# One Macaron block on one core: five changes of order, and the FFN normalisations on ScalarE

## The reference, cut to what matters

```python
x = L0_attn_x                                    # (32, 256, 128) f32
x = x + 0.5 * ffn(layernorm(x))                  # f1
x = x + mamba(layernorm(x))
x = x + 0.5 * ffn(layernorm(x))                  # f2, the same weights
# ffn: logits = x @ Wg + bg; e = argmax over 8 experts
#      y = gelu(x @ W1[e] + b1[e]) @ W2[e] + b2[e]
# mamba: xz = rmsnorm(x) @ in_proj.T -> x_path, z; x_path = silu(causal conv4(x_path) + b)
#      dt, B, C from x_path; dt = softplus(dt @ dt_proj.T + b)
#      h = exp(dt * A) * h + dt * x * B;  y = sum_n h * C + D * x   (16 states, 256 channels)
#      (y * silu(z)) @ out_proj.T + x
```

## Time and profile before

| | us |
|---|---|
| median of 3 runs (lowest, highest) | 1329.93 (1327.08, 1342.4) |
| the profiled execution, its own time | 1330.48 |
| its span, first to last instruction | 1328.7 |
| busy: PE, DVE, ACT, POOL | 1142.2, 1060.7, 857.7, 1067.7 |
| mean granted clock of TensorE | 0.897 |

### The profile page before, as it was taken

How to read it: one execution, slowest core, us unless ns; L and a number is a source line. 1 busy time by engine, 2 the same in 40 slices (tenths; PEclk the granted TensorE clock), 3 DMA queues, 4 the chain that set the end, 5 groups by cost and what they waited for, 6 DMA issues and landing times.

```text
span 1328.7 us, 16290 instructions
## 1 busy us (share of the span) xinstructions
PE 1142.2 (86%) x5188; PEld 579.9 (44%) x5188; DVE 1060.7 (80%) x1713; ACT 857.7 (65%) x1159; POOL 1067.7 (80%) x900
## 2 busy tenths in 40 slices
PE   6886868799999898999989898998989896969588
PEld 3432324244535444544445454454435443524246
DVE  2317989988898988888988988888888889888930
ACT  2327475777768687767768677767768686574531
POOL 1365999998998998889998998899898989897810
PEclk9877979899989998999989999999989997878689
DMA  3060333332141333233141333233141323232000
GB/s 95 0 232 2 135 95 122 111 121 103 59 164 37 135 106 133 90 118 123 58 154 47 135 105 123 100 123 117 42 150 59 135 98 135 96 134 98 0 9 16
DMA packets 60405, 130.02 MB, mean 98 GB/s; under 512 B 7744, under 2 KB 26864, under 8 KB 52128
## 3 DMA queue, kind: packets, MB, share of 16 engines
q1 hardware_dynamic: 60320, 128.98, 28.1%
HBM read 106.94 MB, written 22.02 MB: 97 GB/s over the span
## 4 chain that ended last, share of the span: by engine, by line
PE 59%; DVE 21%; ACT 8%; issue 6%; POOL 5%; SPq 0%; DMA 0%; DVEq 0%; ACTq 0%; POOLq 0%
PE PY L594 17%; PE PH L563 12%; PE G L550 9%; DVE dA L926 8%; PE Y L606 7%; DVE hb L924 4%; PE PH L562 4%; PE G L641 3%; DVE hb L930 3%; PE G L542 2%; PE dA L576 2%; POOL hb L1112 2%; DVE stat L905 2%; ACT hs L751 1%; ACT dA L775 1%
## 5 line engine op out<-in xcount | busy, mean ns | idle before, releaser
L1112 POOL TENSOR_TENSOR hb<-dtx_rep,bs 128x1024 f32<-128x1024 f32 x256 | 598.7, 2359 | 0.0
L926 DVE TENSOR_TENSOR_SCAN dA<-dA,hb 128x512 f32<-128x512 f32 x352 | 429.1, 1219 | 23.8 <-ACT dA L775 16.8
L775 ACT ACTIVATE dA<-dt_rep,A 128x512 f32<-128x512 f32 x512 | 343.7, 690 | 115.9 <-DVE hb L930 97.6
L594 PE MATMUL PY<-W,hs 128*128 128x128 f32 x2048 | 298.6, 289 | 0.0
L594 PEld LDWEIGHTS PY<-W,hs 128*128 128x128 f32 x2048 | 261.9, 196 | 82.8 <-issue 72.1
L731 ACT COPY hs<-PH 128x512 f32<-128x512 f32 x232 | 135.2, 583 | 237.7 <-PE PH L563 235.0
L563 PE MATMUL PH<-xnT,W 128*128 128x512 f32 x464 | 280.5, 688 | 0.0
L930 DVE TENSOR_TENSOR hb<-dA,cs 128x512 f32<-128x512 f32 x352 | 243.5, 692 | 24.8 <-DVE dA L926 0.5
L1120 POOL TENSOR_TENSOR hb<-hb,cs 128x1024 f32<-128x1024 f32 x80 | 188.7, 2359 | 85.0 <-DVE hb L924 85.0
L924 DVE TENSOR_TENSOR_SCAN hb<-dA,hb 128x512 f32<-128x512 f32 x160 | 186.4, 1206 | 8.9 <-ACT dA L775 6.8
L606 PE MATMUL Y<-hb,Sel 128*32 128x512 f32 x1024 | 161.3, 707 | 29.5 <-POOL hb L1120 19.6
(11 more groups left out here) (97 smaller groups left out, 1247.6 us busy)
## 6 DMA issues: line engine op xcount, KB each, us to landing
dtx_rep<-dtx_rows SPq DMA_DIRECT2D x32, 1024.0 KB, 6.5
dt_rep<-dt_rows SPq DMA_DIRECT2D x32, 1024.0 KB, 8.0
bs<-bc_rows SPq DMA_DIRECT2D x64, 256.0 KB, 3.6
cs<-bc_rows SPq DMA_DIRECT2D x64, 256.0 KB, 4.2
dtx_rows<-dtx SPq DMA_DIRECT2D x32, 256.0 KB, 2.5
dt_rows<-dt SPq DMA_DIRECT2D x32, 256.0 KB, 2.6
X<-in_x SPq DMA_DIRECT2D x16, 256.0 KB, 3.0
out<-X SPq DMA_DIRECT2D x16, 256.0 KB, 2.4
```

Of the source, the lines that this page charges most:

```text
L594: last = nc.tensor.matmul(PY[:, P * j:P * (j + 1)], hs[:, w, e, P * j:P * (j + 1)], W2[:, e, :], start=False, stop=e == E - 1 and j == J - 1)
L775: nc.scalar.activation(dA[u % NA][:, :], dt_rep[:, h, g, :], ACT.Exp, scale=A[:, h, g, q:q + 1]).then_inc(decay, 1)
L926: nc.vector.tensor_tensor_scan(a, a, x_in_hb, 0.0, ALU.mult, ALU.add).then_inc(scan, 1)
L1112: nc.gpsimd.tensor_tensor(hb[:, s % HR], dtx_rep[:, h, 2 * m:2 * m + 2, :], bs[:, q, None, :].broadcast_to([P, 2, CH]), ALU.mult).then_inc ...
```

## The change

- The output product goes to Y instead of G0, from (3, 1) to (2, 2); its addition on DVE goes from 3.5 to 3.25, between two units. The first sum of an iteration waits until Y has been read again (`out_read`).
- The one-hot of f1 on DVE goes from 1.0 to 1.25, behind the first unit of slot 1; its transposes on PE from (6, 0) to (5, 1).
- Decay 2 is made in slot 15, ahead of the gelus of f1, and decay 14 in slot 5, ahead of dt0's reads; state_bx(5) in slot 2 instead of 3. x's silu comes before z's. dt0's reads go from 5.5 to 6.0.
- The first product of f1's expert 4 goes to PY, at (10, 3); the places of most other first products and copies move.
- The normalisations of f1 and f2 become four `ACTIVATE` Identity on ACT with scale rstd and bias -m * rstd, a small product more on POOL (`shift`). Their places are 14.5 and 7.5 in the steady plan, and slot 1 in iteration -3.

```diff
-BANK = {"ln_f1": 0, "z0": 0, "out": 0, "bc": 0, "dt0": 0, "gate_f2": 0, "ln_p": 0, "x0": 0,
-        "gate_f1": 1, "z1": 1, "dt1": 1, "oh_f1": 1, "ln_f2": 1, "oh_f2": 1, "x1": 1}
+BANK = {"ln_f1": 0, "z0": 0, "bc": 0, "dt0": 0, "gate_f2": 0, "ln_p": 0, "x0": 0,
+        "gate_f1": 1, "z1": 1, "dt1": 1, "oh_f1": 1, "ln_f2": 1, "oh_f2": 1, "x1": 1, "out": None}
...
 STEADY = Plan(
-    stages=[("ln_f1", 0, 0), ("gate_f1", 0, 2), ("z0", 1, 0), ("z1", 1, 2), ("out", 3, 1), ("bc", 4, 1), ("dt1", 5, 0),
-            ("dt0", 5, 1), ("oh_f1", 6, 0), ("ln_f2", 9, 0), ("gate_f2", 10, 1), ("oh_f2", 12, 0), ("ln_p", 13, 0),
+    stages=[("ln_f1", 0, 0), ("gate_f1", 0, 2), ("z0", 1, 0), ("z1", 1, 2), ("out", 2, 2), ("bc", 4, 1), ("dt1", 5, 0),
+            ("dt0", 5, 1), ("oh_f1", 5, 1), ("ln_f2", 9, 0), ("gate_f2", 10, 1), ("oh_f2", 12, 0), ("ln_p", 13, 0),
             ("x1", 14, 0), ("x0", 14, 1)],
-    w1=[*[(0, e, *at, 3) for e, at in experts((8, 0, 8, 0), (9, 0, 9, 0), (10, 0, 10, 0), (10, 2, 10, 3), (11, 0, 11, 0),
-                                              (12, 0, 12, 0), (13, 0, 13, 0), (14, 1, 14, 0))],
-        *[(1, e, *at) for e, at in experts((15, 0, 15, 0, -1), (15, 1, 15, 0, -1), (15, 3, 15, 3, -1), (0, 2, 0, 1, -2),
-                                           (2, 0, 2, 0, -2), (3, 0, 3, 0, -2), (4, 0, 4, 0, -2), (5, 0, 6, 0, -2))]],
+    w1=[*[(0, e, *at, 3) for e, at in experts((8, 0, 8, 0), (9, 0, 9, 0), (10, 0, 10, 0), (10, 2, 10, 3), (10, 3, 10, 3),
+                                              (11, 1, 11, 0), (12, 0, 12, 0), (13, 0, 13, 0))],
+        *[(1, e, *at) for e, at in experts((14, 1, 14, 0, -1), (15, 0, 15, 0, -1), (15, 1, 15, 1, -1), (15, 3, 15, 3, -1),
+                                           (1, 0, 0, 2, -2), (2, 0, 2, 1, -2), (3, 0, 3, 0, -2), (4, 1, 4, 1, -2))]],
     w2=[*[(0, e, s, 1, 2) for e, s in experts(5, 6, 7, 7, 8, 8, 9, 9)],
         *[(1, e, *at) for e, at in experts((13, 1, -2), (14, 1, -2), (15, 1, -2), (15, 2, -2), (0, 1, -3), (0, 1, -3),
                                            (1, 1, -3), (2, 1, -3))]],
-    act={"silu": 3.0, "bc": 4.5, "dt1": 5.5, "dt0": 5.5, "soft": 6.0, "gelu_f2": 10.5, "ln_f2": 9.5, "ln_p": 13.5,
+    act={"silu": 3.0, "bc": 4.5, "dt1": 5.5, "dt0": 6.0, "soft": 6.0, "norm_f2": 7.5, "norm_f1": 14.5, "gelu_f2": 10.5, "ln_f2": 9.5, "ln_p": 13.5,
          "taps": 14.0, "gelu_f1": 15.5},
-    dve={"gate_f1": 1.0, "gated1": 1.5, "y_f2": [(3.5, -3)], "out": 3.5, "stats_f2": 4.0, "oh_f1": 7.0, "gated0": 9.5,
+    dve={"gate_f1": 1.25, "gated1": 1.5, "y_f2": [(3.5, -3)], "out": 3.25, "stats_f2": 4.0, "oh_f1": 7.0, "gated0": 9.5,
          "y_f1": 10.0, "stats_p": 10.5, "gate_f2": 11.0, "stats_f1": 12.0, "oh_f2": 13.0, "tap01": 15.0, "tap2": 15.5},
-    pool={"root_f2": 5.5, "norm_f2": 6.0, "dt": 7.0, "dtx": 7.5, "root_p": 11.0, "norm_p": 12.0, "root_f1": 12.5,
-          "norm_f1": 13.0},
+    pool={"root_f2": 5.5, "dt": 7.0, "dtx": 7.5, "root_p": 11.0, "norm_p": 12.0, "root_f1": 12.5},
...
 FILL = {
-    -4: Plan(dve={"stats_f1": 0}, pool={"root_f1": 0, "norm_f1": 1}),
+    -4: Plan(act={"norm_f1": 0}, dve={"stats_f1": 0}, pool={"root_f1": 0}),
     -3: Plan(
...
-        act={"ln_f1": 0}, dve={"gate_f1": 0, "oh_f1": 1, "stats_f1": 2}, pool={"root_f1": 0, "norm_f1": 1},
+        act={"ln_f1": 0, "norm_f1": 1}, dve={"gate_f1": 0, "oh_f1": 1, "stats_f1": 2}, pool={"root_f1": 0},
...
-        act={"ln_f1": 0, "ln_p": 6, "taps": 7.5},
+        act={"ln_f1": 0, "ln_p": 6, "norm_f1": 6.5, "taps": 7.5},
...
-        act={"silu": 0, "bc": 2, "dt1": 3, "dt0": 3, "soft": 3.5, "ln_f1": 4.5, "ln_p": 10.5, "taps": 11.5, "gelu_f1": 15.5},
+        act={"silu": 0, "bc": 2, "dt1": 3, "dt0": 3, "soft": 3.5, "ln_f1": 4.5, "ln_p": 10.5, "taps": 11.5, "norm_f1": 12.5, "gelu_f1": 15.5},
...
-    w1=[(1, 3, 0, 0, 0, 0, -2), (1, 4, 0, 0, 0, 0, -2), (1, 5, 0, 1, 1, 0, -2), (1, 6, 1, 1, 2, 0, -2),
-        (1, 7, 2, 1, 3, 0, -2)],
+    w1=[(1, 4, 0, 0, 0, 0, -2), (1, 5, 0, 1, 1, 0, -2), (1, 6, 1, 1, 2, 0, -2), (1, 7, 2, 1, 3, 0, -2)],
...
-    act={"gelu_f2": 3.5, "ln_f2": 4.5},
+    act={"gelu_f2": 3.5, "norm_f2": 4.0, "ln_f2": 4.5},
...
+IN_PY = (0, 4)
+
+EARLY = {(15, 0): 2, (5, 1): 14}
+
+EARLY_B = {2: 5}
...
-                nc.tensor.matmul(PH[:, :], W1[:, e, :], xnT[:, w, :], start=False, stop=True).then_inc(ph_full, 1)
+                if in_py(it.plan, w, e):
+                    it.wait(pe, y_added[0], off - 1, 1, 1)
+                    bank, full = PY, py_full
+                else:
+                    it.wait_unit(pe, ph_free, w, e, 0)
+                    bank, full = PH, ph_full
+                nc.tensor.matmul(bank[:, :], Lm[:, e, :], ohT[:, w, (it.i0 + off) % 2, :], start=True, stop=False)
+                nc.tensor.matmul(bank[:, :], W1[:, e, :], xnT[:, w, :], start=False, stop=True).then_inc(full, 1)
 
...
                         it.wait(pe, y_added[0], 2, 1, 1) if it.has(2) else it.wait(pe, y_added[1], off - 1, 1, 1)
+                        if it.has(3):
+                            it.wait(pe, py_free, 0, 1, 1)
...
                 if k == 0:
-                    it.wait(pe, gated, off, HF, 0)
+                    it.wait(pe, out_read, off - 1, 1, 1)
...
-                    it.wait_free(pe, g_free, "out")
-                    b = BANK["out"]
                     for j in range(J):
                         for h in range(HF):
-                            last = nc.tensor.matmul(G[b][:, P * j:P * (j + 1)], y2[:, h, P * j:P * (j + 1)],
+                            last = nc.tensor.matmul(Y[:, P * j:P * (j + 1)], y2[:, h, P * j:P * (j + 1)],
                                                     Wo[:, h, :], start=h == 0, stop=h == HF - 1)
-                    last.then_inc(g_full[b], 1)
+                    last.then_inc(out_made, 1)
                 xsc = xs[:, (it.i0 + 1) % 2].rearrange("p h b l -> p h (b l)")
...
+            def normalize(it, w, off):
+
+                it.wait(act, rooted[w], off, 1, 1)
+                if it.has(off - 1):
+                    Iteration(it.i0 + off - 1 - OFF[f"ln_f{w + 1}"]).wait_read(act, g_free, f"ln_f{w + 1}")
+                for j in range(J):
+                    last = nc.scalar.activation(xn[:, w, j, :], X[:, it.tiles(off, j, 1), :].rearrange("p o h -> p (o h)"),
+                                                ACT.Identity, scale=rstd[:, w, j:j + 1], bias=shift[:, w, j:j + 1])
+                last.then_inc(normed[w], 1)
...
+                if in_py(it.plan, w, e):
+                    it.wait(act, py_full, 0, 1, 1)
+                    nc.scalar.copy(hs[:, w, e, :], PY[:, :]).then_inc(py_free, 1)
+                else:
+                    it.wait_unit(act, ph_full, w, e, 1)
+                    nc.scalar.copy(hs[:, w, e, :], PH[:, :]).then_inc(ph_free, 1)
 
...
                     it.wait(act, gated, -1, HF, HF)
-                    if it.i0 < 0:
-                        x_silu(it, c)
+                    x_silu(it, c)
                     for h in range(HF) if it.i0 >= 0 else (1, 0):
                         it.wait_full(act, g_full, f"z{h}")
                         b = BANK[f"z{h}"]
                         nc.scalar.activation(zs[:, c, h, :], G[b][:, :], ACT.Silu).then_inc(g_free[b], 1)
-                    if it.i0 >= 0:
-                        x_silu(it, c)
...
-                    if it.has(off):
+                    if it.has(off) and 2 * t not in EARLY.values():
                         make_decay(it, off, 2 * t)
...
-                    stages(it, s + 0.5)
+                    for k in range(2):
+                        if k:
+                            stages(it, s + 0.5)
+                        if (s, k) in EARLY and it.has(off):
+                            make_decay(it, off, EARLY[s, k])
...
-                last = nc.gpsimd.tensor_tensor(rstd[:, w, :], vt[:, w, :], half[:, :], ALU.pow)
+                nc.gpsimd.tensor_tensor(rstd[:, w, :], vt[:, w, :], half[:, :], ALU.pow).then_inc(pool_ln[w], 1)
+                it.wait(pool, pool_ln[w], off, m, 3)
                 if w < 2:
-                    last.then_inc(rooted[w], 1)
+                    nc.gpsimd.tensor_tensor(shift[:, w, :], neg[:, w, :], rstd[:, w, :], ALU.mult).then_inc(rooted[w], 1)
                     return
-                last.then_inc(pool_ln[w], 1)
...
-                    if it.has(off):
+                    if it.has(off) and t not in EARLY_B.values():
                         state_bx(it, off, t)
+                    if it.has(0) and s in EARLY_B:
+                        state_bx(it, 0, EARLY_B[s])
```

51 lines of the change are left out of this document (25 added, 26 removed).

## The result

The changed kernel takes **1356.69 us** (median of 4 runs, 1354.16 to 1362.11) against 1328.51 for the kernel before on the same chip: 1.0178 times, with a 95% interval of 1.0133 to 1.0222. It is slower by 1.8%; I had forecast 1324 and a range up to 1350. The profiled execution has a span of 1355.3 us against 1328.7, at a mean granted clock of 0.884 against 0.897.

The account below looks back on a forecast made before the run. No engine is full; the order between them bounds the loop, forecast at 73.9 us against 75.1. From 1330.48, -12 (loop) - 1 (early) - 5 (tail) + 10 (fill) + 2 (drain) gave 1324.5, median 1324 us, range 1293 to 1350.

Parts of the forecast that it names:

- The clock term: PE's slow stretch behind the hole after the gelus: 0.6 us a period, bounds 0 and 1.7.
- Leg A: Loop part from scan unit 3 on DVE to the first FFN's addition y_f1: 34.1 us, against 35.1 before.
- the transposes' hole: PE stands still 1.6 us ahead of f1's one-hot transposes, until dt1's second read frees the bank.
- The late copy: f1's four activations at 14.5 delay the copies of experts 1 and 2, hence decay 1: 0.9 us a period.
- Legs B and C: Loop from y_f1 to unit 31's end, 28.9 us, then to the next unit 3, 9.4 plus 0.9 for the copy.
- Fill: In iteration -3 ACT's normalisation waits for POOL's root, holding up all eight gelus: +10 us (8 to 12).
- early periods: Periods from 114 to 328 us: leg C gains 0.9, the dt1 wait takes back half to all; -1 us.
- Tail and drain: Tail saves scans and an output product wait, -5 us (-2 to -7); drain has norm_f2 behind both gelus, +2 (0 to 4).
- Rival 3: PE at 1.2 GHz after the 1.6 us hole before the transposes, late slow stretch every period: 1352 us, chance 0.15.
- Rival 1: PE waits for no bank in leg A, no slow stretch or late copy: loop 70.8, time 1293 us, chance 0.15.
- Rival 2: The clock holds behind the 2.55 us hole after the gelus: 0.6 off per period, 1318 us, chance 0.18.
- Rival 4: Nothing of the fill's wait shows, because PE's work there has slack: 1314 us, chance 0.05.

Follow-up runs that it names:

- kernel 6: kernel 1 plus two idle pairs (expert 5's first product of f1 repeated twice into the same bank) per steady iteration: 1326.8 us, ratio 0.998 to before.
- kernel 7: The kernel before plus two idle pairs, repeats of f1's expert 3 first product, per steady iteration: 1338.4 us, ratio 1.006 to before.
- kernel 4: The changed kernel plus one idle pair, f1's expert 5 first product made once more, per steady iteration: 1336.2 us, ratio 1.008 to before.
- kernel 5: kernel 2 plus two idle pairs (f1's expert 5 first product repeated twice) per steady iteration: 1308.7 us, ratio 0.984 to before.
- kernel 9: kernel 5 with the one-hot transposes of f1 back at slot 6: 1284.6 us, ratio 0.967 to before.
- kernel 10: kernel 6 with the one-hot transposes of f1 back at slot 6: 1293.4 us, ratio 0.973 to before.
- kernel 1: The changed kernel with iteration -3's normalisation on ACT moved from slot 1 to 8.5, behind the direct gelus: 1344.0 us, ratio 1.012 to before.
- kernel 2: The changed kernel with both normalisations back on POOL everywhere, leaving the order changes alone: 1326.8 us, ratio 0.998 to before.
- kernel 12: kernel 2 without the product in PY, f1's expert 4 back in its old bank: 1325.1 us, ratio 0.997 to before.
- kernel 11: kernel 2 with the one-hot transposes of f1 back at slot 6, no idle work: 1299.0 us, ratio 0.977 to before.
- kernel 8: kernel 1 with the one-hot transposes of f1 back at slot 6: 1328.1 us, ratio 1.000 to before.
- kernel 3: The kernel before with both normalisations on ACT (iteration -3's at slot 8.5), no order changes: 1348.7 us, ratio 1.014 to before.

## Why the prediction was wrong, by its own steps

**The clock term is the step that failed.** For the slow stretch behind the hole that follows the gelus I gave 0.6 us a period, with 0 and 1.7 as bounds. Without a slow stretch the whole change runs at 73.03 (kernel 6), where my legs sum to 34.1 + 28.9 + 9.4 + 0.9 = 73.3; with the stretches the period of after is 76.07. The term is 76.07 - 73.03 = **3.0 us**, and ten times 2.4 more is 24 us. The fault was in the bounds. I took the difference between the two periods of before, 75.9 and 74.2, as the full price of the slow clock; but the shorter of them also had a loss of 3.7, half of it behind this same hole, and the only period of that kernel without any took 73.0 (kernel 7). The upper end also took it that the stretch behind the hole would be as long as before's, 12 us; with a hole 0.3 shorter it was up to 17. That the clock is what costs the time, and is no mere sign of it, rests on the idle pairs (kernels 4, 5, 6, 9 and 10) and on the table of losses.

**Leg A, the transposes' hole, the output product.** Right: 33.5 us for 34.1, a hole of 1.78 for 1.6; no wait for zs. (The walk puts the second read of dt1 at +17.5 where its own terms add up to 17.3; the transposes came at 591.84 - 574.60 = 17.2.) The hole was on the loop at nearly its full length: 1.1 to 1.9 a period by the table of losses, and 1.5 between kernels 5 and 9 (72.26 and 70.75).

**The late copy.** Right: 0.9 forecast, 0.8 measured, in the place that was named. An activation takes 481 ns (0.50 forecast), four 1.65 us (1.7).

**Legs B and C.** 39.2 forecast without the clock. In the period of kernel 6 in which the clock holds, they take 39.5: right.

**Fill.** +10 forecast (8 to 12), +16.4 in the profile, 12.7 between the medians of after and kernel 1. The wait, the table load of 1.28 and the first gelu were within 0.4 us. What hangs on the wait is 12.0 us by the next iteration's one-hots (50.92 for 38.94), 2 more than forecast. The other 4.5 came between the one-hots of iterations -1 and 0, and are no price of the normalisations that I can show: this stretch took 36.0 to 37.3 us in six kernels and 40.6 to 42.5 in eight, and either place of the normalisation is found in both groups. The whole fill varies as much. With one and the same code for it iteration 0's one-hots were at 112.3, 117.5, 122.9, 123.0 and 123.1 (kernels 2, 12, 5, 9 and 11, normalisations on GpSimd), and with another at 112.5, 117.8, 118.3 and 123.5 (10, 8, 1 and 6, on ScalarE behind the gelus). So the 4.0 of kernel 3 lie within what varies by itself. Of its 7.1 in the early periods, which I had at -1, I can't say more: kernel 10 has only 0.8 more there than kernel 9, kernel 6 has 5.9 more than kernel 5. The Trainium skill's 2.66 us for a table switch ("ScalarE: Activation LUTs", section "What ACT_TABLE_LOAD costs") is not what makes up the difference: in after the load starts at 27.51 and the activation behind it at 28.80, 1.29 us.

**Tail and drain.** -4.1 for -5 and +2.9 for +2: right. The normalisations alone cost about 4 at the end (80.7 in kernel 1, 76.8 in kernel 2).

**The rivals.** Rival 3's second half happened (a late slow stretch in every period), at nearly twice its price; its first half did not: behind the hole of 1.78, where it put PE at 1.2 GHz, the clock stayed at 1.00. Its 1352 is near the measured time with half of the mechanism. Rival 1's loop of 70.8 is what kernel 9 has at a held clock, but only with the transposes moved back, the hole filled and the normalisations on GpSimd. Rival 2 fell: the clock was lower behind the 2.43 in every period. Rival 4 fell with kernel 1, where the fill's wait went and 12 us with it.

The sum with measured terms, in span (what the fill has over the forecast includes the 4.5 that vary by themselves): the forecast was 1328.7 - 6 = 1322.7. Over the nine periods the clock adds 9 x 2.4 = 21.6 and the legs take off 9 x 0.27 = 2.4; the tenth period's forecast gain of 1.2 lies in the stretches beside them; fill +6.4, early periods +3.9, tail +0.9, end +0.9. Together +32.5, or 1355.2, where 1355.3 was measured.
